# Where layer 3's keys and values stand in the queues: all four groups ahead of the adds of layer 2's results, or one group behind each group of adds

## The reference, cut to what matters

```python
x = x + tanh(g_ffn[2]) * L2_ffn(layernorm(x), ...)             # mixture of 8 experts, two per token
x = x + tanh(g_xattn[3]) * L3_xattn(layernorm(x), ctx, ...)    # attention
...
def L3_xattn(queries, context, Wq, bq, Wkv, bkv, Wo, bo):
    q = queries @ Wq + bq
    k, v = split(context @ Wkv + bkv, 2)
    attn = softmax(q @ k.T / 4)      # 16 heads of width 16
    return (attn @ v) @ Wo + bo
```

## Time and profile before

| | |
|---|---|
| median of 3 executions | 1548.8 us (1547.69 to 1549.62) |
| the profiled execution | 1545.74 us |
| its span in the trace | 1543.9 us |
| mean granted TensorE clock | 0.938 of full speed |
| PE busy | 1312.7 us, 85% of the span |
| DVE busy | 960.3 us, 62% |
| ACT busy | 860.8 us, 56% |
| POOL busy | 721.0 us, 47% |

### The profile page before, as it was taken

The page is one execution under the profiler, slowest core; times in us unless marked ns, Lnnn a source line. Parts: engine busy times, 40 slices in busy tenths (PEclk is TensorE's granted clock), DMA queues, the critical chain, the costliest instruction groups (busy, mean ns, idle before and its releaser), DMA issues.

```text
span 1543.9 us, 29425 instructions
## 1 busy us (share of the span) xinstructions
PE 1312.7 (85%) x9497; PEld 955.5 (62%) x9524; DVE 960.3 (62%) x2651; ACT 860.8 (56%) x1718; POOL 721.0 (47%) x859
## 2 busy tenths in 40 slices
PE   2789889998998499999999899839999388995985
PEld 1445479855665289999986556628877245664333
DVE  6779753336985643333337688575544278967787
ACT  2456864434886245455535588535555156875564
POOL 4467440005642577777640564258994426532000
PEclk9999999997999699999999799969999798997998
DMA  9978030049761333343247975125444499710001
GB/s 274 285 153 166 12 100 1 1 130 220 137 140 52 103 123 124 117 149 126 76 148 241 222 129 109 35 89 155 147 132 166 146 259 201 141 28 1 0 14 41
DMA packets 116208, 188.86 MB, mean 122 GB/s; under 512 B 21552, under 2 KB 91824, under 8 KB 110256
## 3 DMA queue, kind: packets, MB, share of 16 engines
q0 software_dynamic: 37696, 105.19, 28.9%
q1 hardware_dynamic: 78368, 81.79, 16.8%
HBM read 128.17 MB, written 50.20 MB: 116 GB/s over the span
## 4 chain that ended last, share of the span: by engine, by line
PE 62%; DVE 14%; DMA 7%; POOL 6%; ACT 5%; issue 5%; SPq 1%; ACTq 0%; DVEq 0%; POOLq 0%
PE PS L1094 8%; PE PS L1253 8%; PE PS L1273 8%; PE PS L1047 8%; PE PS L1051 3%; PE PS L1131 2%; PE PS L1265 2%; DMA qk_parts<-q_parts 2%; PE PS L1074 2%; PE PS L1067 2%; PE PS L1107 2%; POOL weights L818 1%; PE PS L1154 1%; DMA y_tokens<-xng,into 1%; PE PS L911 1%
## 5 line engine op out<-in xcount | busy, mean ns | idle before, releaser
L2152 DVE TENSOR_REDUCE nm<-PS 128x2 f32<-128x512 f32 x384 | 250.3, 676 | 42.2 <-PE PS L1047 40.8
L1047 PE MATMUL PS<-stack 48*128 48x256 f32 x1024 | 212.3, 331 | 38.7 <-issue 10.8
L1047 PEld LDWEIGHTS PS<-stack 48*128 48x128 f32 x1024 | 151.6, 204 | 121.0 <-issue 61.6
L1051 PE MATMUL PS<-stack 49*128 49x256 f32 x1024 | 203.9, 322 | 1.0 <-ACT probs L1576 0.6
L1273 PE MATMUL PS<-weights,hh 128*128 x936 | 189.5, 292 | 3.8 <-DVE hl L2481 3.7
L1253 PE MATMUL PS<-weights,xh 128*128 x468 | 169.9, 418 | 11.3 <-DVE xl L2467 5.4
L1576 ACT ACTIVATE probs<-PS 128x512 f32<-128x512 f32 x256 | 145.0, 595 | 36.4 <-PE PS L1074 15.1
L709 POOL DMA_DIRECT2D stack<-mt x128 | 73.1, 571 | 185.4 <-ACT mt L1585 183.8
L1576 ACT ACTIVATE xng<-PS 128x512 f32<-128x512 f32 x256 | 145.3, 595 | 21.8 <-PE PS L1074 12.5
L1273 PEld LDWEIGHTS PS<-weights,hh 128*128 128x128 f32 x936 | 152.7, 193 | 5.4 <-issue 4.9
L1051 PEld LDWEIGHTS PS<-stack 49*128 49x128 f32 x1024 | 143.5, 195 | 10.5 <-ACT probs L1576 4.3
(11 more groups left out here) (335 smaller groups left out, 3079.9 us busy)
## 6 DMA issues: line engine op xcount, KB each, us to landing
stack<-qk_parts POOLq DMA_DIRECT2D x120, 256.0 KB, 4.1
stack<-qk_parts POOLq DMA_DIRECT2D x136, 128.0 KB, 3.7
qk_parts<-stack SPq DMA_DIRECT2D x32, 512.0 KB, 6.6
qk_parts<-q_parts SPq DMA_DIRECT2D x26, 512.0 KB, 5.3
weights<-W_dram POOLq DMA_DIRECT2D x12, 1024.0 KB, 7.0
wide<-ctxT_dram SPq DMA_DIRECT2D x16, 512.0 KB, 8.0
wslot<-y_tokens SPq DMA_DIRECT2D x16, 512.0 KB, 7.4
weights<-W_dram POOLq DMA_DIRECT2D x12, 512.0 KB, 5.1
```

The costliest lines, as they stand in the source:

```text
L1047: mm = pe.matmul(PS[:, u % 3, to], nat_q[:, at], nat_k, start=True, stop=True)
L1051: mm = pe.matmul(PS[:, 3 + v % 3, to], key_k[:, at], key_q, start=(l > 0 or half == 0), stop=(l > 0), skip_group_check=(l == 0))
L2152: nc.vector.tensor_reduce(nm[:, j % 2, at:at + 2], PS[:, (2 * t + h) % 3, :].rearrange("p (q n) -> p q n", q=2), AX.X, ALU.max, negate=Tru ...
```

## The change

The diff moves calls in three queues. No instruction is added or removed, and no size changes.

- PE: `keys_values(3, 3)` comes in front of `transposes(6, 0)` (behind it before).
- ACT: `keys(3, g)` and `values(3, g)` of all four groups come first. Before, the keys of group g + 1 stood in front of the root of group g, and the values behind it.
- DVE: `keys_low(3, g)` of all four groups come in front of the adds of layer 2's results. Before, group 0 stood there, and group g + 1 between the variances and the scales of group g.

For layer 2 (`l == 2` on PE and ACT, `l == 1` in DVE's loop, where the next layer is meant) the order is that of before.

```diff
@@ PE, project(l), l >= 2
                     u = 2 * l
-                    keys_values(l, 0)
-                    keys_values(l, 1)
-                    keys_values(l, 2)
+                    for g in range(GROUPS - 1):
+                        keys_values(l, g)
+                    if l == 3:
+                        keys_values(l, 3)
                     transposes(u, 0)
-                    keys_values(l, 3)
+                    if l == 2:
+                        keys_values(l, 3)
                     queries(l, 0)
@@ ACT, project(l), l >= 2
                     u = 2 * l
-                    keys(l, 0)
-                    values(l, 0)
+                    for g in range(GROUPS if l == 3 else 1):
+                        keys(l, g)
+                        values(l, g)
                     for g in range(GROUPS - 1):
-                        keys(l, g + 1)
+                        if l == 2:
+                            keys(l, g + 1)
                         group_roots(u, g)
-                        values(l, g + 1)
+                        if l == 2:
+                            values(l, g + 1)
                         if g == 1:
                             features(l, 0)
                         normed(u, g)
@@ DVE, sparse(l)
-                keys_low(l + 1, 0)
+                for g in range(GROUPS if l == 2 else 1):
+                    keys_low(l + 1, g)
                 if l == 2:
                     dve.wait_ge(ln_x, 1)
                 for g in range(GROUPS):
@@
                     group_variances(2 * l + 2, g)
-                    if g + 1 < GROUPS:
+                    if g + 1 == GROUPS:
+                        queries(l + 1, 0)
+                    elif l == 1:
                         keys_low(l + 1, g + 1)
-                    else:
-                        queries(l + 1, 0)
                     group_scales(2 * l + 2, g)
```

## The result

The changed kernel takes 1567.12 us (median of 4 executions, 1557.03 to 1576.56) against 1548.24 us for the kernel before (4 executions). The ratio is 1.0121, with a 95% interval from 1.0087 to 1.0155: 13 to 24 us slower, around the forecast of 19.2 (the two medians lie 18.9 apart).

The account below looks back on a forecast made before the run. The prediction took a late key store, queued behind the result loads, as the bound. Adds 24.96 us later, less 5.72 us for three groups, 0 for the tail: +19.2 us on 1548.8, so 1568.0 us, range 1564.5 to 1571.5.

Parts of the forecast that it names:

- The likeliest case: The forecast as worked out: adds start later, groups run faster, tail unchanged, 19.2 us slower in sum; chance 0.82.
- The buffer of key group 2: ACT's third high part stays at 1242.05 us, since its buffer is freed by a key store queued behind SP's result loads.
- Key group 3: PE's matmuls start at 1244.90 after a pause and take 5.19 us at the low clock; other end 3.67.
- Start of the adds: DVE's adds of layer 2's results start behind all four low parts, at 1252.75 in place of 1227.79: 24.96 us later.
- 6.66 us per group: On DVE, a group without a low part takes 6.66 us, not 7.62; three groups take 19.98 us, not 25.70.
- The tail: From the last group's adds to layer 3's first scores: 20.3 us, practically unchanged, with 19 and 23 as ends.
- The rival of the tail: PE's last eight query matmuls may run at the higher clock: only 16.2 to 17.7 us slower; chance 0.10.
- a sign of being wrong: The forecast was to count as wrong if under 20 us lay between the last adds and the first scores.
- The other side: Faster: all four low parts fit in DVE's idle time before the result loads land, 5.7 us gained; chance 0.02.
- The range: 1564.5 to 1571.5 us, from the ends of key group 3's matmuls and the tail, plus 1 us of spread either way.

Follow-up runs that it names:

- A: The changed kernel run again with no edit, beside more executions of the kernel before: ratio 1.0104 to the kernel before.
- B: Kernel before, with key groups 0 to 2 ahead of the adds on DVE and ACT, group 3 left behind: ratio 1.0075.
- C: Kernel before, with key groups 0 and 1 ahead of the adds on DVE and ACT, groups 2 and 3 left: ratio 1.0025.
- F: Changed kernel, with SP's key stores of groups 0 and 1 moved ahead of its wait for the last scatters and the result loads: ratio 1.0004.
- G: F, with POOL also waiting for the adds of group 1 before it reads the first keys back: ratio 0.9983 to the kernel before.
- H: Changed kernel, with a second buffer for the key parts of groups 2 and 3 of layer 3: ratio 0.9983, and 0.9988 once more.
- J: Changed kernel, with 35 useless matmuls on PE in the wait before key group 3: ratio 1.0131; a first run with 70 gave 1.0275.

## Why the prediction was right

The likeliest case came about, by its own steps. That it met the time so closely is in part luck: two errors of a microsecond cancelled in the first trace, and A gives 16 us over the kernel before in place of 19, with an interval from 10.5 to 21.5.

- *The buffer of key group 2.* ACT's third high part was released by the store, 17.2 us after the first result load's issue; the kernel before gave 18.3 us. This is 1.2 us in the change's favour that I had as fixed, and B and C have 17.2 as well. F, G and H show that this store sets the loss: early, or with its buffer replaced, the loss is gone.
- *Key group 3.* I took 8.1 us from its predecessor's low part to its own, with 5.19 for the matmuls. It took 9.07, since they took 6.18. The bounds, 3.67 and 5.19, were both too low: after the pause PE ran the eight matmuls in 5.1 to 6.3 us in these traces, 6.18 and 6.30 in the changed kernel's two. The granted clock in the changed kernel was 0.50 (1.2 GHz) for some 5 of the 6.2 us: it is 0.50 up to 1257, 0.68 from there to 1258 and 1.00 behind that (the number before the last two of each line), and the matmuls end at 1258.76:

```profile
1252.00:1256.00 4.00, 3.42 (x4) 1.50 (x5) 0.43 (x1) 0.00 (x0) 0.04 (x1) 0.50 1.12 170
1256.00:1257.00 1.00, 1.00 (x3) 0.36 (x2) 0.00 (x0) 0.00 (x0) 0.00 (x0) 0.50 1.10 318
1257.00:1258.00 1.00, 1.00 (x3) 0.50 (x2) 0.00 (x0) 0.00 (x0) 0.00 (x0) 0.68 1.07 370
1258.00:1259.00 1.00, 1.00 (x4) 0.57 (x3) 0.00 (x0) 0.21 (x1) 0.00 (x0) 1.00 0.92 324
```

- *Start of the adds.* 28.85 us after the issue against 29.01 worked out (4.05 + 24.96). The two errors above cancelled.
- *6.66 us per group.* Measured 6.66 and 6.67, in every kernel with all keys in front, but for the first group of F, which halted for a load.
- *The tail.* 20.35 us for 20.3, though not as I had it. The sixteen query matmuls took 10.16 us, not 8.6, so that ACT's high part behind them started 14.4 us after the last adds, not 12.9; the last eight ran at the high clock, 3.70 us for 5.14, and gave that back. The rival of the tail was right about these eight. In A the sixteen took 8.52 us and the eight 3.70, and the tail was 18.71 us, less than the 20 that I had named as a sign of being wrong. The 20.28 us of before were at the long end too: the five other traces with fewer than four groups in front ran the eight in 3.70 us and had tails of 18.8 to 19.4. The change may cost some tenths of a microsecond here, but with 18.7 and 20.4 us for the same kernel that is not shown.
- *The other side.* I had put the point from which it decides at the last low part being over 5.72 us behind the landing of the results, and its gain at 5.7 us. G and H are that case: 5.6, 5.3 and 5.7 us in the stretch, though not in the whole time. I had given no thought to what an earlier store would set free on POOL.
- *The range.* Its terms add up to 3.8 us below and 3.7 above, where I wrote 3.5 for both. The measured time lies inside either way.

The page Perfetto Trace Analysis of the Trainium skill, section Matmul Optimizations, asks for matmuls back to back. The changed kernel gave key group 2 that (3.60 us by its timeline, at 1214.05) and took it from key group 3; J sets its worth at 2.6 us, against 19 for the wait.

## What to carry to other kernels

Before independent work is moved into an engine's idle time, follow each of its instructions to the buffer that it writes and to the DMA that frees it, and see where that DMA stands in its queue. With two buffers only two of the four groups fit in front, and an engine that works in order turned the third one's wait into everybody's. When such a wait is then removed by sending the store sooner, look at what else the store was holding back: here a read-back that landed on top of the loads that mattered. And a stretch that gets 5 us shorter in the trace is not yet a faster kernel: here the whole executions showed at most some 2 us of it, which their spread does not tell from nothing.

## What the runs showed of the hardware

- Four read-backs of 768 KB in all, issued by POOL beside SP's eight result loads, stretched the landing of the second load to 9.6 us in F; with POOL held back in G, DVE had both loads of group 0 without a halt, 4.05 us after the first issue.
- Beside stores of 2 MB (F and G) POOL's scatters started 1.82 us apart in the mean, against 1.59 to 1.70 in the ten traces without an early store. In F and G the two longest gaps, of 2.6 to 2.7 and 3.3 us, fell while the stores travelled, but a gap of 2.7 us (H) and one of 2.9 (J with 70) came without any.
- The same instructions reach the same point with a spread of 9.5 us in a program of 1550 us. A stretch counted from its own first event repeated within 1.2 us in two executions of the changed kernel. One trace laid over another by the time axis would have put the cost of the change at 28 us (the first scores) or 31 (the spans).
